# A four-layer block on one core: the steps behind the mLSTM heads taken batch by batch, the router's weights folded into the output projection, and a region of rows for each expert

## The reference

```python
# 1. mLSTM attention, 8 heads: q, k 16 wide a head, v 32 wide
h = scan(...)                        # numerator and qn for each token and head
h = h_num / (max(|qn|, exp(-m)) + EPS)
h = sigmoid(x @ Wog.T) * (multihead_norm(h) * gamma)
y = h @ Wout.T
# 2. mixture of 16 experts, 4 a token, weights normalised over the 4
logits = x @ router_w.T + expert_bias
top_w, top_idx = top_k(softmax(logits), 4)
y = sum over the 4 of top_w * (silu(x @ gate[e]) * (x @ up[e])) @ down[e]
# 3. gated linear attention, 16 heads
# 4. mixture of 32 experts, 8 a token, computed for all experts
```

## Time and profile before

| | |
|---|---|
| Time, median of 3 runs | 710.92 us (701.72 to 715.23) |
| Time of the profiled execution | 710.83 us |
| Its span, first to last instruction | 709.0 us |
| Mean granted clock of PE | 0.868 |
| PE busy | 551.6 us (78%) |
| DVE, ACT, POOL busy | 366.9, 231.2, 266.8 us |
| Head units | about 30 to 88 us |
| Tail and dispatch | 88 to 133 us |
| Scatter | 133 to 177 us |
| 47 expert tiles | 177 to 296 us |

### The profile page before, as it was taken

The page is one execution under the profiler, slowest core; times in us unless marked ns, Lnnn a source line. Parts: engine busy times, 40 slices in busy tenths (PEclk is TensorE's granted clock), DMA queues, the critical chain, the costliest instruction groups (busy, mean ns, idle before and its releaser), DMA issues.

```text
span 709.0 us, 10743 instructions
## 1 busy us (share of the span) xinstructions
PE 551.6 (78%) x3351; PEld 472.6 (67%) x3351; DVE 366.9 (52%) x956; ACT 231.2 (33%) x587; POOL 266.8 (38%) x243
## 2 busy tenths in 40 slices
PE   8889885000999999700488869669999999999994
PEld 5656574000898988600354438659999999999994
DVE  4554664500344444337479986596644444444445
ACT  4643523000455555501360103313333333333334
POOL 4462110376267894077118860040314124044000
PEclk9995987555899999955599996869999999999998
DMA  8942000122266775233100003001022020100001
GB/s 260 377 135 69 0 1 1 45 104 101 78 189 188 230 234 185 83 101 101 36 0 1 0 22 113 1 1 67 1 67 68 1 68 15 51 0 0 0 0 59
DMA packets 42266, 54.12 MB, mean 76 GB/s; under 512 B 5729, under 2 KB 37234, under 8 KB 42226
## 3 DMA queue, kind: packets, MB, share of 16 engines
q1 hardware_dynamic: 25330, 32.34, 14.5%
q10 hardware_dynamic: 13536, 12.33, 5.5%
q0 software_dynamic: 3360, 8.93, 3.9%
HBM read 36.02 MB, written 17.56 MB: 76 GB/s over the span
## 4 chain that ended last, share of the span: by engine, by line
PE 65%; DVE 11%; POOL 10%; issue 5%; DMA 4%; ACT 4%; POOLq 0%; ACTq 0%; SPq 0%; DVEq 0%
PE PS L1381 45%; POOL FA L629 4%; POOL xg L601 4%; PE PS L1577 3%; DMA FA<-xg 2%; PE PS L1478 2%; PE PS L1456 2%; DVE FA L1335 2%; PE PS L1612 1%; DVE PS L1319 1%; PE PS L1552 1%; PE PS L1636 1%; POOL FA L644 1%; PE PS L1441 1%; DMA FA<-in_w0T 1%
## 5 line engine op out<-in xcount | busy, mean ns | idle before, releaser
L1381 PE MATMUL PS<-EW,XH 128*128 128x384 f32 (+2 forms) x732 | 208.4, 366 | 6.0 <-DVE SQ L1169 4.4
L1381 PEld LDWEIGHTS PS<-EW,XH 128*128 128x128 f32 x732 | 126.2, 192 | 10.4 <-DVE SQ L1169 4.7
L1381 PE MATMUL PS<-EW,XL 128*128 128x384 f32 (+2 forms) x366 | 129.1, 353 | 0.0
L1169 DVE SCALAR_TENSOR_TENSOR SQ<-SIL,CW,PS 128x96 f32<-128x96 f32 x256 | 69.0, 311 | 115.7 <-ACT SIL L772 114.6
L1381 PE MATMUL PS<-EW,EHH 128*128 128x256 f32 (+1 forms) x476 | 101.7, 289 | 0.2
L772 ACT ACTIVATE SIL<-PS 128x192 f32<-128x192 f32 x128 | 42.6, 332 | 160.7 <-PE PS L1381 160.7
L1381 PE MATMUL PS<-EW,EHL 128*128 128x256 f32 (+1 forms) x286 | 80.1, 280 | 0.0
L1381 PEld LDWEIGHTS PS<-EW,EHH 128*128 128x128 f32 (+1 forms) x476 | 78.0, 188 | 1.1 <-issue 0.6
L1381 PEld LDWEIGHTS PS<-EW,XL 128*128 128x128 f32 x366 | 70.2, 192 | 2.2
L568 POOL TENSOR_TENSOR round_mark<-round_mark 128x1 f32<-128x1 f32 x10 | 2.2, 218 | 183.2 <-PE PS L1381 131.8
L1612 PE MATMUL PS<-ident,FA 128*128 128x128 f32 x94 | 19.0, 286 | 50.1 <-DMA FA<-xg 50.1
(11 more groups left out here) (294 smaller groups left out, 1098.3 us busy)
## 6 DMA issues: line engine op xcount, KB each, us to landing
EG<-in_gateup SPq DMA_DIRECT2D x16, 448.0 KB, 4.1
xg<-EQ SPq DMA_DIRECT2D x1, 6016.0 KB, 26.0
FA<-xg ACTq DMA_DIRECT2D x47, 128.0 KB, 2.4
yg<-FA ACTq DMA_DIRECT2D x47, 128.0 KB, 2.3
ED<-in_down SPq DMA_DIRECT2D x16, 224.0 KB, 4.6
EG<-in_gateup SPq DMA_DIRECT2D x4, 768.0 KB, 4.4
FA<-in_gateup SPq DMA_DIRECT2D x4, 768.0 KB, 4.6
ED<-in_down SPq DMA_DIRECT2D x4, 384.0 KB, 5.7
```

The lines of the kernel that those rows point to most:

```text
L1169: ins = dve.scalar_tensor_tensor(out=HH[:, pos % 2, h:h + W], in0=SIL[:, s, j * W:(j + 1) * W], scalar=c, in1=bank(s)[:, I + j * W:I + (j ...
L1381: ins = pe.matmul(o, l, r, start=start and i == 0, stop=stop and i == n - 1, skip_group_check=True)
```

## The change

- Slots: each expert has its own region of 1024 rows in `xg`, so the row of a pick is known from the tokens up to its own batch. `xg` has 16384 rows instead of 6016, and the fill with zeros goes to ACT's queue, behind its first tanh. The tables of tiles get the row at which each tile starts (`tile_rows`); ACT reads them into registers, 16 at a time, and loads its tiles from there. The rows of `yg` stay packed; `pack_slots` works out the packed slots for the gather.
- Tail by batch: the steps behind the heads run for two tiles at a time between the units, until unit 50 (the constants in the diff are the offsets from the first unit of a batch; those of PE count pairs); banks 6 and 7 serve two batches in turn. Roots are no longer taken by ACT but by `rsqrt` on DVE (a guess from the bits and three Newton steps, 10 small operations).
- The mean of squares is taken from the undivided heads, with the denominator put into the epsilon.
- Router: the product of `WO0` with the router's weights is made once (`fold_router`) and stands as 16 more columns in `WO0H`, `WO0L`; the logits come out of the same products as the projection, from the residual and the heads, and are scaled with the layernorm's root afterwards. No second turn and split of `XB` for the router.
- Softmax weights of the 4 picks are taken from the 4 largest logits.
- Expert tiles: the copy of the output goes from ACT to DVE (`outputs`).

```diff
+        EVAC_AT, COPY_AT, DEN_AT, SCALE_AT, PARTS_AT = 9, 12, 13, 14, 17
+        NORM_AT, X_AT, TOP_AT, PICK_AT, SLOT_AT = 21, 22, 22, 23, 25
+        TOKENS_AT, TURN_AT, PROJECT_AT, RANKS_AT = 5, 8, 10, 12
+        UNITS = (B - 1) * NH0 + SLOT_AT + 1
...
+            gate(0)
+            gate(1)
+            pool.wait_ge(xg_zero, 16)
+            scatter(0)
+            gate(2)
+            scatter(1)
+            gate(3)
             split(BGH, BGL, bg[:]).then_inc(w_split, 1)
...
+            scatter(2)
+            scatter(3)
...
+            act.wait_ge(zero_set, 1)
+            act.dma_start(xg.rearrange("(n p) d -> p n d", p=P),
+                          EQ[:].rearrange("p t e -> p (t e)").unsqueeze(1).broadcast_to([P, E0 * NT, D])
+                          ).then_inc(xg_zero, 16)
...
+            def rsqrt(x, y, a, b):
+                ch.link(dve.tensor_scalar(y.bitcast(I32), x.bitcast(I32), -0.5, 1597463007.0, ALU.mult, ALU.add))
+                for _ in range(3):
+                    ch.link(dve.tensor_tensor(a, y, y, ALU.mult))
+                    ch.link(dve.scalar_tensor_tensor(out=b, in0=x, scalar=-0.5, in1=a, op0=ALU.mult, op1=ALU.mult))
+                    ch.link(dve.scalar_tensor_tensor(out=y, in0=b, scalar=1.5, in1=y, op0=ALU.add, op1=ALU.mult))
...
+            def scale_heads(b):
+                two = slice(2 * b, 2 * b + 2)
+                v, e2 = hs[:, two, 0:NH0], hs[:, two, NH0:2 * NH0]
+                dve.wait_ge(sq_done, b + 1)
...
+                ch.link(dve.scalar_tensor_tensor(out=v, in0=v, scalar=NH0 / D, in1=e2, op0=ALU.mult, op1=ALU.add))
+                y = hr[:, two, 0:NH0]
+                rsqrt(v, y, hr[:, two, NH0:2 * NH0], e2)
+                dve.wait_ge(og_ready, b + 1)
...
+            def pair_norm(b):
+                two = slice(2 * b, 2 * b + 2)
+                dve.wait_ge(y_done, 2 * b + 2)
+                for t in (2 * b + 1, 2 * b):
+                    ins = dve.bn_stats(st[:, t, :], bank(7 - t % 2)[:, 0:D])
...
+                rsqrt(rv[:, two], rstd[:, two], t1[:, two, 0], t1[:, two, 1])
...
+                for at, step in ((DEN_AT, denominators), (SCALE_AT, scale_heads), (PARTS_AT, pair_lo),
+                                 (NORM_AT, pair_norm), (TOP_AT, pair_top), (PICK_AT, pair_picks),
+                                 (SLOT_AT, pair_slots)):
+                    b = batch_at(u, at)
+                    if b is not None:
+                        step(b)
...
+            def heads_to_tokens(b):
+                pe.wait_ge(ao_evac, 2 * (b + 1))
+                if b == 0:
+                    pe.wait_ge(fold_ready, 1)
+                else:
+                    pe.wait_ge(lo_done, b)
+                if b >= 2:
+                    pe.wait_ge(slots_ready, b - 1)
...
+            def project_pair(b):
+                if b == 0:
+                    pe.wait_ge(ld_x, 16)
+                else:
+                    pe.wait_ge(slots_ready, b)
+                if b + 1 < B:
+                    pe.wait_ge(sq_done, b + 2)
+                pe.wait_ge(lo_done, b + 1)
+                for t in (2 * b + 1, 2 * b):
+                    o = bank(7 - t % 2)
+                    c = slice(t * P, (t + 1) * P)
+                    pe.matmul(o[:, 0:D], ident[:], XA[:, t, :], start=True, stop=True, skip_group_check=True)
+                    for k in range(KD):
+                        pe.matmul(o[:, D:DR], XT[:, k, c], WRT[:, k, 0:E0], start=False, stop=False, skip_group_check=True)
+                    lhs = [(HTH[:, k, c], HTL[:, k, c]) for k in range(KD)]
+                    mm3(o[:, 0:DR], lhs, ws(WO0H, WO0L, 0, DR), False, True).then_inc(y_done, 1)
...
             def load_tile(i):
-                act.dma_start(XG[:, i % 4, :], xg[i * P:(i + 1) * P, :]).then_inc(xg_ld[i % 4], 16)
+                if i % ROWS_AT_ONCE == 0:
+                    _, at = nc.values_load_multi_w_load_instructions(tile_rows[0:1, i:i + ROWS_AT_ONCE], engines=(mybir.EngineType.Activation,),
+                                        min_val=0, max_val=E0 * NT - 1)
+                    rows.update(enumerate(at, i))
+                act.dma_start(XG[:, i % 4, :], room[bass.ds(rows[i], 1)].rearrange("o p d -> p (o d)")
+                              ).then_inc(xg_ld[i % 4], 16)
```

More of the change, by code:

```diff
@@ new lines, in pair_top @@
+            def pair_top(b):
+                dve.wait_ge(lg_ready, 2 * b + 2)
+                for t in (2 * b, 2 * b + 1):
+                    ins = dve.max(top[:, t, :], LG[:, t, 0:E0])
+                ch.link(ins)
+                for t in (2 * b, 2 * b + 1):
+                    ins = dve.max_index(tix[:, t, :], top[:, t, :], LG[:, t, 0:E0])
+                ch.link(ins)
+                two = slice(2 * b, 2 * b + 2)
+                ch.link(dve.tensor_copy(tif[:, two, :], tix[:, two, :]))
@@ new lines, in pair_picks @@
+            def pair_picks(b):
+                two, shape = slice(2 * b, 2 * b + 2), [P, 2, E0, TOP0]
+                with nc.allow_low_precision(reason="the picks are zero or one"):
+                    ch.link(dve.tensor_tensor(picks[:, two], iota_e[:, 0:E0].unsqueeze(1).unsqueeze(3).broadcast_to(shape),
+                                              tif[:, two, 0:TOP0].unsqueeze(2).broadcast_to(shape), ALU.is_equal))
+                    dve.tensor_reduce(chosen[:, 2 * b * E0:(2 * b + 2) * E0].rearrange("p (t e) -> p t e", t=2),
+                                      picks[:, two], AX_X, ALU.add).then_inc(mask_ready, 1)
@@ new lines, in ranks @@
+            def ranks(b):
+                pe.wait_ge(mask_ready, b + 1)
+                pe.wait_ge(x_act, 2 * b + 2)
+                tiles = lambda c0, n: bank(7)[:, c0 * E0:(c0 + n) * E0].rearrange("p (n e) -> p n e", n=n)
+                taken = lambda t: chosen[:, t * E0:(t + 1) * E0].unsqueeze(1)
+                last = 1 if b == B - 1 else 0
+                pe.matmul(bank(7)[:, 0:2 * E0], earlier[:], chosen[:, 2 * b * E0:(2 * b + 2) * E0], start=True, stop=False,
+                          skip_group_check=True)
+                for t in range(2 * b):
+                    pe.matmul(tiles(0, 2 + last), onesb, taken(t).broadcast_to([P, 2 + last, E0]), start=False, stop=False,
+                              skip_group_check=True)
+                pe.matmul(tiles(1, 1 + last), onesb, taken(2 * b).broadcast_to([P, 1 + last, E0]), start=False, stop=False,
+                          skip_group_check=True)
+                if last:
+                    pe.matmul(tiles(2, 1), onesb, taken(2 * b + 1), start=False, stop=False, skip_group_check=True)
+                pe.matmul(tiles(0, 2), onesb[0:1, :], room_first.unsqueeze(1).broadcast_to([1, 2, E0]), start=False,
+                          stop=True, skip_group_check=True).then_inc(rank_mm, 1)
@@ L1591, in moe_pe @@
                 pe.wait_ge(dn_done, base + m.total)
-            def ranks():
-                pe.wait_ge(mask_ready, 1)
-                pe.matmul(bank(3)[:, 0:NT * E0], earlier[:], chosen, start=True, stop=False, skip_group_check=True)
-                for t in range(NT):
-                    out = bank(3)[:, (t + 1) * E0:(NT + 1) * E0].rearrange("p (n e) -> p n e", e=E0)
-                    ins = pe.matmul(out, onesb, chosen[:, t * E0:(t + 1) * E0].unsqueeze(1).broadcast_to([P, NT - t, E0]),
-                                    start=False, stop=(t == NT - 1), skip_group_check=True)
-                ins.then_inc(rank_mm, 1)
             def sparse_pe():
```

420 lines of the change are left out of this document (262 added, 158 removed).

## The result

Median of 14 runs 718.65 us (715.22 to 725.82); the kernel before, on the same chips, 713.89 (701.72 to 719.07). The ratio of the two is 1.0163, 95% interval [1.0129, 1.0197]: 1.6% slower, 23 us above the forecast of 696 and 6 above the range. The ratio compares fast runs alone, and of the 14 runs of the kernel before 8 lie more than 1.5% above its fastest and stay out of it: by it the change costs about 11.5 us, by the medians of all runs 4.8. The profiled execution took 717.6 us.

A forecast was written before the change was run, and what follows sets the result against it. The wait from last head product to first expert tile was taken as the bound: loop end 113 + tail 35 + scatters and reads 14.5 = 162.5 instead of 177.4, so about 696 us, range 682 to 713 for 8 in 10.

The forecast's parts named there:

- The registers: Row-number reads: 1 us before the first tile, 0 before tiles 16 and 32; at the other end 13 in all.
- rival 3: Row numbers read by sixteen single register loads: 13 us more, 708 us; chance 0.08.
- The loop end: End of the head loop: 113 us instead of 88, bounds 104 and 122, with 10 us at low clock per period.
- Unit 16: In the head loop, this unit was to start near 57.6 us instead of 55.8.
- the clusters: Units 21 to 23 and 29 to 31 of the head loop: TensorE waits 7 us for DVE in each.
- Behind the loop: Remaining batch steps from loop end to the last slots: 31.5 to 38 us, taken as 35.
- `gate(3)`: GpSimd's gate behind the loop: ready near +15 us, wanted by DVE at +17, so covered with little to spare.
- The tile stage: The expert tiles: unchanged at 2.37 us a tile.
- the output copy: Moving each tile's copy from ACT to DVE costs nothing, covered by TensorE; uncovered, up to 19 us.
- The fill: Zeroing `xg`, 16.0 MB instead of 6.0: landed by 83 us, before a first scatter near 85, so hidden, barely.
- The sum: Whole kernel: span 709.0 - 15 = 694, about 696 us with the profiled execution's 1.8 over its span.
- the rivals: Stops grow, 709 (0.20); steps hide better, 684 (0.18); sixteen single loads, 708 (0.08); fill holds ACT, 745 (0.05).

The follow-up runs named there:

- e1: The changed kernel with the first sixteen row numbers read before the wait for the scatters: 713.88 us, ratio 1.0094 to the kernel before.
- e7: The changed kernel with its groups of sixteen row numbers read without range checks: 707.80 us, ratio 1.0026 to the kernel before.
- e9: The changed kernel with products of zeros on TensorE sized to its stops in the head loop: 713.15 us, ratio 1.0101 to the kernel before.
- e4: The changed kernel with two Newton steps instead of three in the reciprocal square root: 712.58 us, ratio 1.0071 to the kernel before.
- e15: e10 with two Newton steps instead of three in the reciprocal square root: 689.80 us, ratio 0.9789 to the kernel before.
- e8: The changed kernel with single row reads, three before the scatter wait, and GpSimd's split of bg between scatters 2 and 3: 707.21 us, ratio 1.0008.
- e3: The changed kernel with the copy of each tile's output back on ScalarE: 721.36 us, ratio 1.0166 to the kernel before.
- e6: The kernel before with only the larger fill, 16 MB instead of 6 MB, issued on ScalarE's queue: 708.30 us, ratio 1.0055.
- e13: The kernel before with 4, 2 and 2 products of zeros ahead of the scores of units 12, 20 and 28: 706.21 us, ratio 1.0042.
- e12: The kernel before, unchanged, run once more for a second profile: 718.90 us, a single run.
- e14: e10 with turn, projection, norm, picks and slots of each batch eight units later: 702.07 us, ratio 0.9981 to the kernel before.
- e10: The changed kernel with single unchecked row reads, e8's order and e9's products of zeros: 703.08 us, ratio 0.9909 to the kernel before.
- e11: e10 with more products of zeros behind the head loop and ahead of the first tile: 703.17 us, ratio 0.9925 to the kernel before.
- e2: The changed kernel with one row number read ahead of each tile load instead of sixteen at a time: 708.70 us, ratio 1.0010.
- e5: The changed kernel with 40 products of zeros on TensorE at each of three stops in the head loop: 744.57 us, ratio 1.0565.

## Why the prediction was wrong

**The registers: the step that failed.** The prediction put them at "1 and 0, since ACT loads tiles three ahead". Measured: 5.3 us before the first tile, and a stop of ScalarE of 4.9 at tile 16, the like at tile 32. The two stops reached TensorE as 5.1 us of waiting, and it was at the low clock for 11.7 us of the stage instead of 6.7: together 6.4 us. e1 took the first away (4.8 us), e7 the checks of all three (11 by the medians, 10 by the ratios), and e7's stage is back at 112.7. About 11 of the 22 us between the forecast and the profiled execution are this. Its upper end, 13 in all, and rival 3 had the size, but by another mechanism, sixteen loads; it is one load and sixteen checks. "Three tiles ahead" protects TensorE from a late load, but not from ScalarE, which owes every tile three operations: a stop of two tiles' length reached TensorE as 2.6 us each time. The 298 ns of a single read agree with the 312 ns taken, and not with the floor of about 600 ns of the Trainium skill (DMA: Bandwidth & Descriptors, Latency and other measured facts).

**The loop end** was right, 113.4 for 113, in part by luck, since its parts were not all right. Unit 16 began at 54.6, before the 57.6 foreseen, but its scores came only at 60.3, behind a stop of 4.8 us (57.7 in the kernel before); the clusters stopped TensorE 6.2 and 12.5 us, not 7 and 7; it had 28 us at the low clock from there on, not 20. That the clock is its own cost, e9 shows (6 us). That VectorE's steps are the stops, the traces say (it is the releaser of all but one), and e4 and e15 fit: 3.1 us less of the steps gave 1.0 with the clock low, 4.8 with it kept up (the missing stop is in these 4.8, so they don't prove the one-for-one).

**Behind the loop** it was 39.5 us to the last slots for 35: above the upper bound of 38. TensorE's clock was 0.59 there (`project_pair(2)` took 6.2 us), and `pair_norm(2)` ran into GpSimd's gate and split:

```profile
127.77 1.27 POOL L623 TENSOR_TENSOR OGATE<-OGATE,HC 128x512 f32<-128x512 f32 x1
127.90 1.18 DVE L1120 TENSOR_SCALAR rv<-mv 128x2 f32<-128x2 f32 x1
...
130.46 0.16 DVE L1057 TENSOR_TENSOR t<-rstd 128x2 f32<-128x2 f32 x1
```

1.18 us for 0.17, and it ended with GpSimd's operation. That is in line with what the Trainium skill says (SBUF — State Buffer, Who interferes with whom) of a tensor_scalar in a two-port mode beside a GpSimd instruction; the trace doesn't show the mode. The scatters did no such thing to the norm of batch 3, which took 4.3 us beside them. How the 4.5 us divide between the two is not shown, and e8, which took the split away, brought no earlier slots. `gate(3)` itself was in time.

**The tile stage** was not "unchanged at 2.37 us a tile": by the registers, as e7 shows; for the output copy no cost can be seen (e3), as taken. **The fill** was hidden, within 1 to 6 us that e6 shows and no trace places.

**The sum** once more: 696 + 0.4 (loop) + 4.5 (behind) + 5.3 (reads 4.4 over the 1 taken, 0.9 from slots to the first scatter) + 6.4 (stage) + 5.1 (behind the tiles) = 717.7, the profiled execution's 717.6 but for rounding. The 5.1 are no step of the prediction: the one profiled execution of before was as quick behind the tiles as e13, and 5 us quicker than e6 and e12, as told above.

**Of the rivals** none came true as written. The one that I should have written is the plain one: the loop pays what the tail saves. Loop end to first tile fell from between 86 and 90 us (four executions) to 59.3, or 54.2 in e8; the loop end rose from between 81 and 95 to 113.4. I read this so: a kernel whose serial tail is VectorE's gains from interleaving only what VectorE had free. e14 puts that at 3.5 us for one batch, or 6 to 7.7 if the stop is no part of it.

**Open:** the few us of e6; what lowers the clock in the loop of the kernel before (e13); the 5 us behind the tiles; and the stop below.

## What to carry to other kernels

Count what an engine's sequencer does around a read of registers, range checks included, and place it where that engine waits anyway; "loaded some tiles ahead" covers the data, not the engine that reads the numbers. A stop of TensorE has two prices, the stop and the low clock behind it, and a little dead work sized to the stop buys back the second. Take a second profile of the kernel before, where its clock is mixed, before a sum is made against the first, and compare a stretch that no edit touches: where it differs, compare ratios and not times.

## What was not expected of the hardware

In 8 of the 13 profiled executions of the change and its variants VectorE and ScalarE stand still together for 4.0 to 7.9 us while batch 1's norm is due. They start again within 0.1 us of each other, but for e9, e10 and e11 (0.7 to 2.1 apart). In the change TensorE's projection, for which the norm waits, is done at 97.5 by its records; the releaser is an event that the trace doesn't show:

```profile
102.45 0.47 ACT L789 ACTIVATE EW<-PS,ATF 128x256 f32<-128x256 f32 x1 [7.89 <-remote]
102.49 0.77 DVE L1115 BATCH_NORM_STATS2 st<-PS 128x6 f32<-128x256 f32 x2 [6.51 <-remote]
```

The 5 us from 97.5 to 102.5 hold back all that VectorE does next, and so are probably 5 of the 12.5 us of the last stop above. In e4, e14 and e15 the norm starts 0.1 us behind the projection, without such a stop. In e7 and e8 the trace names the projection as releaser, but there too both engines start together, 1.4 and 1.5 us behind it, at 102.6 as in the change; their projection came 3.6 to 3.8 us later, behind a longer stretch at the low clock, and their loop ended no later for it (113.6 and 113.5). In six executions (the change, e1, e2, e3, e7, e8) they start 0.2 to 0.5 us behind the end of GpSimd's `gate(2)`, in e5, e9, e10 and e11 before that, so the gate alone doesn't explain it. No edit was aimed at it, and its cause is not known.
